# Attention stage of a two-layer metaformer: other distances in tiles between its engines, another order on the DMA queue, a third buffer

## What is computed

```python
# layer 3, linear attention (its key/value sums come from a sampled pass before this stage)
x = x + _L1_conv_ref(_ln_c(x), ...)
#   Q = elu(q_w @ ln(x) + q_b) + 1
#   Z = 1 / (Q . sum(K) + EPS);  out = proj(Q @ KV * Z) + proj_b
# layer 4: experts that each choose 8 tokens
t = _to_tokens(x)
t = t + _L1_ffn_ref(_ln_t(t), ...)
#   logits = gate_w @ ln(t);  softmax over all tokens;  top 8 tokens of each of 32 experts
```

## Time and profile before

| | us |
|---|---|
| median of 3 runs | 2359.74 (2351.72 to 2361.3) |
| the profiled execution | 2354.4 |
| its span | 2352.6 |
| attention stage in it | 1433 to 2112 |

### The profile page before, as it was taken

The page is one execution under the profiler, slowest core; times in us unless marked ns, Lnnn a source line. Parts: engine busy times, 40 slices in busy tenths (PEclk is TensorE's granted clock), DMA queues, the critical chain, the costliest instruction groups (busy, mean ns, idle before and its releaser), DMA issues. The chain is left out here.

```text
span 2352.6 us, 26577 instructions
## 1 busy us (share of the span) xinstructions
PE 1914.9 (81%) x6218; PEld 792.0 (34%) x6218; DVE 1248.2 (53%) x1960; ACT 1311.3 (56%) x2139; POOL 1324.4 (56%) x1089
## 2 busy tenths in 40 slices
PE   4999999999995599999999956888888888853300
PEld 1333333333331344545455423222222222212200
DVE  2788888888885001203011053688888888862000
ACT  3777777777762243343434333788888888840000
POOL 3999999999993000001000031888888888831476
PEclk9999999999997799999999977999999999975555
DMA  4688888888855700906427033677787777643010
GB/s 148 180 253 246 247 246 257 246 243 244 247 186 161 321 0 23 396 9 247 181 92 300 0 143 117 207 246 241 243 244 243 243 243 243 194 143 76 2 2 2
DMA packets 111839, 429.83 MB, mean 183 GB/s; under 512 B 44080, under 2 KB 49104, under 8 KB 66640
## 3 DMA queue, kind: packets, MB, share of 16 engines
q1 hardware_dynamic: 91936, 423.79, 56.2%
q10 hardware_dynamic: 15536, 4.28, 1.1%
q0 software_dynamic: 4224, 0.20, 0.2%
HBM read 257.91 MB, written 170.01 MB: 182 GB/s over the span
## 5 line engine op out<-in xcount | busy, mean ns | idle before, releaser
L454 ACT ACTIVATE tap_products<-xn,kk 128x512 f32<-128x512 f32 x384 | 275.1, 718 | 165.1 <-POOL x_and_products L485 159.5
L753 PE MATMUL pss<-region,wT 128*128 (+1 forms) x688 | 357.2, 608 | 0.7 <-ACT warm_state L802 0.7
L385 PE MATMUL pst<-xn,taps 128*128 128x512 f32 x768 | 350.7, 592 | 0.0
L485 POOL TENSOR_TENSOR x_and_products<-tap_products,x_and_products 128x512 f32<-128x512 f32 x256 | 326.4, 1275 | 41.7 <-POOL x_and_products L485 3.6
L809 ACT ACTIVATE region<-pss,bn 128x256 f32 x256 | 178.3, 696 | 263.7 <-PE pss L755 263.7
L1374 POOL TENSOR_SCALAR exp_q<-exp_q 128x512 f32<-128x512 f32 x128 | 196.1, 1532 | 190.5 <-ACT exp_q L1333 190.5
L755 PE MATMUL pss<-region,vT 128*128 (+1 forms) x496 | 258.6, 610 | 0.0
L839 DVE TENSOR_TENSOR diff<-reached,true_state 128x512 f32<-128x512 f32 x4 | 2.8, 692 | 462.9 <-POOL true_state L825 462.9
L543 DVE SCALAR_TENSOR_TENSOR pst<-xn,kk,pst 128x512 f32<-128x512 f32 x256 | 192.0, 750 | 95.1 <-PE pst L385 94.8
L825 POOL COPY true_state<-region 128x512 f32<-128x512 f32 x4 | 4.1, 1037 | 400.1 <-ACT region L809 400.1
L385 PEld LDWEIGHTS pst<-xn,taps 128*128 128x128 f32 x768 | 145.2, 189 | 184.9 <-issue 184.4
(11 more groups left out here) (239 smaller groups left out, 3193.2 us busy)
## 6 DMA issues: line engine op xcount, KB each, us to landing
rstd_wide<-rstd_scratch SPq DMA_DIRECT2D x128, 512.0 KB, 7.3
x_ring<-in_x SPq DMA_DIRECT2D x32, 1024.0 KB, 5.2
x_scratch<-x_ring SPq DMA_DIRECT2D x32, 1024.0 KB, 4.3
xl_scratch<-wx SPq DMA_DIRECT2D x32, 1024.0 KB, 8.7
region<-xl_scratch SPq DMA_DIRECT2D x32, 1024.0 KB, 15.8
x_ring<-x_scratch SPq DMA_DIRECT2D x32, 1024.0 KB, 5.9
rstd_of_channels<-rstd_scratch SPq DMA_DIRECT2D x64, 512.0 KB, 9.2
x_transposed<-x_squares SPq DMA_DIRECT2D x64, 512.0 KB, 4.8
```

What stands on the lines that cost most here:

```text
L385: m = pe.matmul(wide(pst[g % 2]), taps[:, n * P:(n + 1) * P], tap_rows(g, t), start=(n == 0), stop=(n == len(PE_TAPS) - 1))
L454: act.activation(prod[:, n, :, :], tap_rows(g, t), ACT.Copy, scale=kk[:, t:t + 1]).then_inc(products, 1)
L485: pool.tensor_tensor(xr[:, g % XR, :], prod[:, n, :, :].rearrange("p r w -> p (r w)"), xr[:, g % XR, :] if n else x_tile(g), ALU.add).then ...
L753: pe.matmul(pss[par][h][:, :], wT[:, :], at(b, n, h), start=True, stop=False)
```

## The change

- Lags: `QUERY` 8 to 9, `QSCALE` 9 to 10, `QMAP` 10 to 12, `DENOM` 11 to 13, `BYZ` 12 to 14, `ATTEND` and `X3` 13 to 15, `SQ3` and `TURN` 14 to 16, the rounds' statistics 4 and 18 to 5 and 20, the gates and what follows them by 2, `LOAD` -6 to -5.
- Buffers: `q_map` 5 to 6, the squares (4, 5) to (6, 6), the turned half blocks 2 to 3.
- Order within a step: PE does its statistics last instead of first. ACT squares the mean first, one step after the PE (it was the same step), and computes the inverse as the last thing of a step, with the squares of x between logarithm and inverse. POOL multiplies by the inverse first, then clips, then maps. SP issues load, store of x, the broadcasts, the turned half block and at last the small writes to DRAM.

```diff
-            QSLOTS = 5
-            SQSLOTS = (4, 5)
+            QSLOTS = 6
+            TSLOTS = 3
+            SQSLOTS = (6, 6)
...
-            LOAD, SQ2, QUERY, QSCALE, QMAP, DENOM, BYZ, ATTEND, X3, SQ3, TURN = -6, 0, 8, 9, 10, 11, 12, 13, 13, 14, 14
-            STATS = (4, 18)
-            GATE, GSCALE, BEST, BEST_AT, EXPSUM = 22, 23, 26, 27, 28
+            LOAD, SQ2, QUERY, QSCALE, QMAP, DENOM, BYZ, ATTEND, X3, SQ3, TURN = -5, 0, 9, 10, 12, 13, 14, 15, 15, 16, 16
+            STATS = (5, 20)
+            GATE, GSCALE, BEST, BEST_AT, EXPSUM = 24, 25, 28, 29, 30
...
                 for t in range(LOAD, STEPS_D):
-                    for l in range(2):
-                        if (k := block_at(t, STATS[l] + 2)) is not None:
-                            rstd_to_dram(l, k)
+                    if (k := block_at(t, LOAD)) is not None:
+                        load(k)
+                    if (k := block_at(t, X3 + TPB)) is not None:
+                        store_x3(k)
                     if (k := block_at(t, STATS[0] + 3)) is not None:
                         rstd_to_channels(k)
                     if (k := block_at(t, STATS[1] + 3)) is not None:
                         rstd_to_experts(k)
-                    if (k := block_at(t, LOAD)) is not None:
-                        load(k)
-                    if (k := block_at(t, X3 + TPB)) is not None:
-                        store_x3(k)
-                    if (h := pair_at(t, TURN + 2)) is not None:
+                    if (h := pair_at(t, TURN + 1)) is not None:
                         store_xt(h)
+                    for l in range(2):
+                        if (k := block_at(t, STATS[l] + 2)) is not None:
+                            rstd_to_dram(l, k)
...
                 for t in range(0, STEPS_D):
                     for l in range(2):
+                        if (k := block_at(t, STATS[l] + 1)) is not None:
+                            square_mean(l, k)
+                    if (g := tile_at(t, SQ3)) is not None:
+                        square_x3(g)
+                    for l in range(2):
                         if (k := block_at(t, STATS[l] + 2)) is not None:
                             rsqrt(l, k)
-                    for l in range(2):
-                        if (k := block_at(t, STATS[l])) is not None:
-                            square_mean(l, k)
                     if (k := block_at(t, EXPSUM)) is not None:
                         exp_logits(k)
+                    if (g := tile_at(t, QSCALE)) is not None:
+                        exp_query(g)
+                    if (g := tile_at(t, DENOM)) is not None:
+                        log_denominator(g)
+                    if (g := tile_at(t, SQ2)) is not None:
+                        square_x2(g)
                     if (g := tile_at(t, DENOM)) is not None:
                         inverse_denominator(g)
-                    if (g := tile_at(t, QSCALE)) is not None:
-                        exp_query(g)
-                    if (g := tile_at(t, SQ3)) is not None:
-                        square_x3(g)
-                    if (g := tile_at(t, SQ2)) is not None:
-                        square_x2(g)
...
                 for t in range(0, STEPS_D):
+                    if (g := tile_at(t, BYZ)) is not None:
+                        query_by_inverse(g)
                     if (g := tile_at(t, QMAP)) is not None:
                         clip_exp(g)
-                    if (g := tile_at(t, BYZ)) is not None:
-                        query_by_inverse(g)
                     if (g := tile_at(t, QMAP)) is not None:
                         map_query(g)
```

More of the change, by code:

```diff
@@ L1088, in build_program @@
             qz = sb("q_z", [P, 2, TILE], F32, ph)
-            xt = sb("x3_squares", [P, 2, HALFB], F32, ph)
+            xt = sb("x3_squares", [P, TSLOTS, HALFB], F32, ph)
             lg = sb("logits", [P, 2, HALFB], F32, ph)
@@ L1103, in build_program @@
             x3_stored = [S(f"x3_stored{r}") for r in range(SEMS)]
-            xt_stored = [S(f"xt_stored{r}") for r in range(2)]
+            xt_stored = [S(f"xt_stored{r}") for r in range(TSLOTS)]
             rstd_out = [S(f"rstd3_out{r}") for r in range(2)]
@@ L1218, in _ @@
                         rstd_to_experts(k)
-                    if (k := block_at(t, LOAD)) is not None:
-                        load(k)
-                    if (k := block_at(t, X3 + TPB)) is not None:
-                        store_x3(k)
-                    if (h := pair_at(t, TURN + 2)) is not None:
+                    if (h := pair_at(t, TURN + 1)) is not None:
                         store_xt(h)
+                    for l in range(2):
+                        if (k := block_at(t, STATS[l] + 2)) is not None:
+                            rstd_to_dram(l, k)
                 for k in range(NBLK - SEMS, NBLK):
                     sp.wait_ge(*stored_x3(k))
-                for r in range(2):
-                    sp.wait_ge(xt_stored[r], 16 * NBLK)
+                for h in range(2 * NBLK - TSLOTS, 2 * NBLK):
+                    sp.wait_ge(xt_stored[h % TSLOTS], 16 * (h // TSLOTS + 1))
             @blk.tensor
@@ L1288, in _ @@
                         attend(g)
+                    if (g := tile_at(t, QUERY)) is not None:
+                        query(g)
                     if (p := pair_at(t, GATE)) is not None:
                         gate(p)
-                    if (g := tile_at(t, QUERY)) is not None:
-                        query(g)
+                    for l in range(2):
+                        if (k := block_at(t, STATS[l])) is not None:
+                            stats_of(l, k)
             @blk.scalar
@@ L1339, in inverse_denominator @@
                     act.activation(lnd[:, :], pd[:, :], ACT.Ln, bias=eps_z).then_inc(lnd_done, 1)
+                def inverse_denominator(g):
                     act.wait_ge(lnd_done, g + 1)
@@ L1437, in turn_x3 @@
                     dve.wait_ge(x3_ready, g + 1)
-                    if g % 2 == 0 and h >= 2:
-                        dve.wait_ge(xt_stored[h % 2], 16 * (h // 2))
-                    dve.transpose(xt[:, h % 2, cols_of(g % 2)], x_tile(g)).then_inc(turned, 1)
+                    if g % 2 == 0 and h >= TSLOTS:
+                        dve.wait_ge(xt_stored[h % TSLOTS], 16 * (h // TSLOTS))
+                    dve.transpose(xt[:, h % TSLOTS, cols_of(g % 2)], x_tile(g)).then_inc(turned, 1)
                 def scale_logits(p):
```

5 lines of the change are left out of this document (2 added, 3 removed).

## The result

The changed kernel takes 2397.72 us in the median of 4 runs (2395.53 to 2401.21), the kernel before 2359.38 (4 runs): ratio 1.017, 95% interval 1.0144 to 1.0196. It is slower, as forecast, but by 1.7% instead of 0.7%. The forecast was 2377 with a range of 2346 to 2397, so the median lies just above the range. The profiled execution took 2397.09 us, 42.7 more than that of before, with a span of 2395.3.

What follows compares the result with a forecast made beforehand. The prediction took a PE-DVE chain, two laps a block, to bound the kernel before. It summed 22 - 5 + 1 = +18 us onto the profiled 2354.4, giving 2372, and forecast a median of 2377 us, range 2346 to 2397.

Steps and rivals of the forecast that it cites:

- the lap of PE and DVE: Chain from clamp through PE's sums and attended value back to DVE: 9.8 us, two laps a block, removed by the change.
- PE's wait for the variance: PE's second sum waits 1.21 us for DVE's clamped variance; if Step 1 is right, below 0.5 us a block.
- step 2: SP's small write behind large transfers makes `rb3` and the query scaling late: 20.5 us a block, +22 us.
- Step 1: New chain PE, ACT, POOL, back to PE, closes in one block without slack: period at least 19.8 us.
- PE's wait for `q_map`: Sign of Step 1: PE waits for POOL's map at a denominator once a block, by about 2 us.
- Step 3: Pipeline's fill and drain: earlier first scalings give -5 us in the fill, the drain costs +1.
- The drain: Pipeline's end, with as many steps as before: +1 us.
- Rival 1: Step 1 decides alone, as transfers overlap or the small write slips through: period 19.8, 2361 us; chance 0.36.
- Rival 2: Faster: the chain has unseen slack, `rb3` lands in time, PE's 17.2 us decides; period near 17.8, about 2310; chance 0.14.

Runs made afterwards that it cites:

- experiment 1: Changed kernel with only SP's order altered: both broadcasts first, small writes behind load and store, these issued one step later; ratio 1.0095 to the kernel before.
- Experiment 10: Kernel of Experiment 3 with ACT's inverse put directly behind the logarithm, ahead of the squares of x; ratio 1.0016 to the kernel before.
- experiment 6: Changed kernel with denominator and all behind it one step later, SP's order of experiment 1, store at step 20; ratio 1.0003 to the kernel before.
- experiment 4: Kernel before the change, given only the change's order on SP, with the old lags; ratio 0.9982 to the kernel before.
- experiment 2: Changed kernel with two more query products on PE in phase 3, written over by the real one; ratio 1.0118 to the kernel before.
- Experiment 3: Changed kernel with both the SP order of experiment 1 and the repeated query products of experiment 2; ratio 1.0009 to the kernel before.
- 7: Kernel of experiment 6 with the store two steps later and the experts' broadcast behind the small write of l = 0; ratio 0.992 to the kernel before.
- 12: Kernel of Experiment 10 with SP's queue in order of need as well; ratio 1.0007 to the kernel before.
- experiment 5: Changed kernel with denominator and all behind it one step later, SP's order and the store's step kept; ratio 1.0253 to the kernel before.
- 11: Kernel of 7 with ACT's inverse put directly behind the logarithm, ahead of the squares of x; ratio 0.9935 to the kernel before.

## Why the prediction was off

**What bounded the kernel before** was read rightly: the lap of PE and DVE is gone, and PE's wait for the variance with it. The gain never came, because two other laps of about 20 us stood ready. That the change is slower was forecast for a reason that held (step 2); that it is slower by 1.7% needed a cost that the prediction had put at nothing.

**Step 1** held. Forecast 19.8 us, measured 19.55 in the first block of the changed kernel and in the ten clean blocks of experiment 1. Its sum was 0.25 too long, and it is in fact 0.05 under the 19.60 of before. Experiment 10 showed that the chain runs through ACT's inverse, experiment 6 that the later denominator opens it.

**Step 2** held: the small write stands behind the load and all that follows it, its `rb3` is late, and the price is shared by two blocks. From the load at 1652.38 to the scaling at 1671.53 there are 19.15 us, forecast 18.9 (the 19.3 less the 0.4 from gate to load). The clean blocks take 20.36 us in the mean, forecast 20.5. 25 x (20.36 - 19.60) is 19.0 us, forecast 22. Experiment 1 took it away, experiment 4 showed that it needs the new lags. In experiment 2 two blocks took 41.4 us, forecast 41.1.

**The step that failed** is the price of PE's wait for `q_map`: the clock was missing from the sum. The prediction's last paragraph foresaw that PE would wait once a block for `q_map`, "by about 2 us", and put no price on it beyond the wait itself. Eight blocks of 22.30 instead of 20.36 are 15.5 us; by the 1.7 us that PE is busy longer in the two blocks read above, 13.6 of it is PE's own work at the lower clock. Experiment 3 against experiment 1 shows that this is the clock and that the wait brings it; experiment 2 shows that another long wait of PE does the same. The stretch read in the earlier trace rows had a granted clock of 1.00 because PE's longest waits were short; I took that clock for given.

**Step 3** was right on the first scalings and wrong on what they are worth. They did start earlier:

```profile
1453.56 0.69 DVE L1425 TENSOR_TENSOR query<-ps_query,rstd_of_channels 128x512 f32<-128x512 f32 x1 [11.13 <-DMA rstd_of_channels<-rstd_scratch]
...
1467.29 0.69 DVE L1425 TENSOR_TENSOR query<-ps_query,rstd_of_channels 128x512 f32<-128x512 f32 x1 [7.30 <-DMA rstd_of_channels<-rstd_scratch]
...
1523.48 0.69 DVE L1425 TENSOR_TENSOR query<-ps_query,rstd_of_channels 128x512 f32<-128x512 f32 x1 [4.19 <-PE ps_query L1259]
```

That is 5.3 and 7.9 us, of which 2.8 are no gain of this stage, since it began that much earlier (its first load is issued at 1430.45, before at 1433.21). The other 2.6 and 5.1 are the 2.5 and 5 of the forecast. But the first mark moved by 0.1 only: counted from the start of the stage it comes 2.6 us later than before, where the forecast had it 5 earlier. The gain is lost on the way to the mark. The 4.19 us of the third row are one such place; that step 2's loop has begun by then is my reading, and no run shows it. The drain was given +1 and took +7.5. Its clock is lower (mean 0.83 from 2068.69 to 2152.98, where before it was 0.88), but PE's busy time in it is only 2.2 us longer (55.3 for 53.1). In experiment 2, with PE kept busy, the drain is 77.1 us, and in experiment 1, with the other order on the queue, 79.3 (76.8 before). Each of the two edits takes most of the 7.5 away in one profile, so how much of it is the clock stays open.

**The sum.** Forecast 18. Against it, steady part without the clock -3, clock +15.5, up to the first mark +4.9 (-0.1 for -5), drain +6.5, after the stage +0.8: 42.7.

Rival 1 was that step 1 decides alone: that is experiment 1's clean blocks, and would have been right without the queue, though even then the clock would have cost 25 us. Rival 2's 17.8 us a block was never reached; the best version, with both laps opened, has 19.11, so its bound of 17.2 for PE was not near enough to decide anything.

## What to carry to other kernels

A longer distance in tiles removes a wait between two engines and may close a longer chain through four; write each hand-over with its slack in steps, follow it until it comes back to its start, and compare the sum with the period. On a queue that issues in order, a small write that someone waits for belongs ahead of the megabytes that nobody waits for, and its reader behind no other reader's wait. Where a new wait falls on PE, price the matmuls behind it at half the clock as well, and look for lags that move the wait to another engine before filling it with idle work.

## What the runs showed of the hardware

- A PE wait of 2.35 to 2.67 us once in about 20 us brought the granted clock down in 8 of 25 blocks (15 of 25 in experiment 1), for 1.7 us each. The Trainium skill (TensorE: Matmul & The Clock Gate, "A second HAM failure mode") tells of small idles between groups of matmuls that make the clock go to and fro. In these traces it goes to and fro as well, behind single waits of about 2 us and more.
- Over the profiles of all fourteen kernels, between the marks of blocks 0 and 25, each of the 75 falls of the clock lies between 0.8 us before and 1.5 us after the end of a PE wait of 1.97 us or more, whether PE waited for POOL, ACT or DVE. Where no wait of PE was over 1.82 us (the kernel before and experiments 3, 4, 7, 10 and 12) the clock did not fall. One of 2.98 us had no fall either (experiment 5). Which of the long waits tip it is not shown by these runs.
- Two products more per block on PE made a kernel faster (experiments 2 and 3).
- A small write behind three MB on one queue was complete only with them: 12.1 us from the load's issue at 1652.38 to that of its reader at 1664.51. Experiment 6 had 3.5 MB in 14.0 us (1710.25 to 1724.29). Both are some 260 GB/s, nearer to the 246 of the earlier trace rows than to the 475.
- In the runs of experiments 3, 4 and 7 to 11 the kernel before took 2480 us, on two chips, and 2354 to 2360 in the others. One of these two chips is also that of experiment 12, where it took 2354, so it isn't a fixed property of the chip. In experiment 4's profile the attention stage's marks span 567.9 us, as before (566.7), and what follows the last mark 366.9 instead of 241.5, with the same busy time on each engine (PE 38.2 us in both, POOL 118.6 for 118.4). What the tail waits for there was not looked into. Each ratio has both kernels in the same such case.
